# Other orders for the last two batches, and one batch's down projections in another PSUM bank, in a gated cross-attention and expert kernel

## What is computed

```python
def xattn(x, ctx, ...):                     # 16 heads of 8 channels
    y  = softmax(causal(q @ k.T * scale)) @ v        # self attention
    y += softmax(qc @ kc.T * scale) @ vc             # against the context
    return y @ Wp + bp

def ffn(x, ...):                            # 16 experts, hidden size 64
    combine = route(x @ router_weight.T)    # sigmoid, best 2 of 4 groups, best 4 experts, weights
    for e in range(16):
        out += combine[:, e] * ((silu(x @ w_gate[e].T) * (x @ w_up[e].T)) @ w_down[e].T)

x = x + tanh(g_xattn) * xattn(layernorm(x), ctx)
x = x + tanh(g_ffn) * ffn(layernorm(x))
```

## Time and profile before

| | us |
|---|---|
| median of 3 runs | 349.12 |
| the 3 runs | 349.02 to 356.06 |
| the profiled execution | 349.41 |
| its span | 347.6 |
| busy in the span: PE, DVE, ACT, POOL | 318.1, 256.4, 196.2, 151.1 |

### The profile page before, as it was taken

One profiled execution on the slowest core, in us unless ns is written; L12 is line 12 of the kernel. 1 busy time (PEld: TensorE's weight loads), 2 busy tenths in 40 slices (PEclk: granted clock), 3 DMA queues, 4 the chain that ended last, 5 costly groups with the idle time before them and its releaser, 6 DMA issues.

```text
span 347.6 us, 8679 instructions
## 1 busy us (share of the span) xinstructions
PE 318.1 (92%) x3186; PEld 247.7 (71%) x3186; DVE 256.4 (74%) x639; ACT 196.2 (56%) x399; POOL 151.1 (43%) x176
## 2 busy tenths in 40 slices
PE   1579599989999999999999999999999999978696
PEld 0455365666687788778887888787888787856665
DVE  4238666868898888988798888888889854748742
ACT  2433356767667765687637765675666467532041
POOL 3884061404470588047633494318410722903422
PEclk9856759999999999999999999999999999989999
DMA  4269674688563855537655365077156005214000
GB/s 123 68 183 188 146 194 115 145 209 187 199 151 103 184 131 149 143 96 151 147 139 133 88 172 140 20 152 183 34 124 141 0 18 90 37 50 88 16 1 15
DMA packets 32889, 40.45 MB, mean 116 GB/s; under 512 B 3440, under 2 KB 29824, under 8 KB 30368
## 3 DMA queue, kind: packets, MB, share of 16 engines
q1 hardware_dynamic: 32004, 38.46, 46.7%
q10 hardware_dynamic: 844, 1.45, 1.7%
HBM read 29.84 MB, written 7.45 MB: 107 GB/s over the span
## 4 chain that ended last, share of the span: by engine, by line
PE 76%; DVE 7%; DMA 6%; SPq 5%; POOL 2%; issue 2%; ACT 1%; POOLq 0%; DVEq 0%
PE bank L918 15%; PE bank L846 14%; PE bank L825 8%; PE bank L943 7%; PE bank L800 7%; PE bank L803 6%; PE bank L822 5%; DMA k_stack<-tri_k 4%; SPq L427 2%; PE bank L893 2%; DVE row_max L1011 2%; PE bank L861 2%; PE bank L852 2%; SPq L426 1%; PE bank L956 1%
## 5 line engine op out<-in xcount | busy, mean ns | idle before, releaser
L1011 DVE TENSOR_REDUCE row_max<-bank 128x2 f32<-128x512 f32 (+1 forms) x224 | 146.9, 686 | 43.0 <-PE bank L803 24.9
L709 ACT ACTIVATE probs<-bank 128x512 f32<-128x512 f32 x224 | 127.5, 595 | 57.5 <-PE bank L825 27.7
L918 PE MATMUL bank<-xn2T,w_pairs_sb 128*128 128x256 f32 x256 | 68.0, 392 | 1.5 <-issue 0.9
L846 PE MATMUL bank<-probs,v_ext 128*32 128x256 f32 (+1 forms) x1024 | 57.2, 365 | 0.0
L626 POOL TENSOR_TENSOR f_h<-f_h,comb 128x512 f32<-128x512 f32 x32 | 40.3, 1273 | 36.1 <-DMA comb<-c_scr 20.4
L803 PE MATMUL bank<-k_stack,q_stack 72*128 72x256 bf16 x256 | 49.9, 284 | 2.7 <-DVE row_max L1011 2.1
L918 PEld LDWEIGHTS bank<-xn2T,w_pairs_sb 128*128 128x128 f32 x256 | 44.7, 193 | 8.3 <-issue 2.8
L825 PE MATMUL bank<-q_stack,k_stack 73*128 73x256 bf16 x256 | 49.2, 284 | 1.0 <-DMA q_stack<-shiftT 0.9
L412 POOL TENSOR_TENSOR rest<-proj,part 128x512 f32<-128x512 f32 x14 | 16.2, 1160 | 74.7 <-ACT part L682 74.6
L846 PEld LDWEIGHTS bank<-probs,v_ext 128*32 128x32 f32 x1024 | 30.0, 112 | 19.9 <-issue 4.7
L800 PE MATMUL bank<-k_stack,q_stack 121*128 121x128 bf16 (+1 forms) x384 | 39.1, 231 | 2.4 <-DMA k_stack<-tri_k 1.9
(11 more groups left out here) (113 smaller groups left out, 367.9 us busy)
## 6 DMA issues: line engine op xcount, KB each, us to landing
k_stack<-k_scr SPq DMA_DIRECT2D x45, 192.0 KB
q_stack<-q_scr SPq DMA_DIRECT2D x14, 576.0 KB
comb<-c_scr SPq DMA_DIRECT2D x14, 512.0 KB, 6.7
q_scr<-part SPq DMA_DIRECT2D x46, 64.0 KB
k_scr<-part SPq DMA_DIRECT2D x46, 64.0 KB
x_in<-in_x SPq DMA_DIRECT2D x8, 128.0 KB, 2.4
w_pairs_sb<-in_w_pairs SPq DMA_DIRECT2D x1, 1024.0 KB, 7.8
out<-y_out SPq DMA_DIRECT2D x8, 128.0 KB, 1.9
```

The costliest lines, as they stand in the source:

```text
L709: nc.scalar.activation(probs[:, seq % NP, :], exp_bank[s % 2][:, :], ACT.Exp).then_inc(exp_done, 1)
L846: last = pe.matmul(pv_bank[32 * n:32 * n + VW, col + q0:col + T], v[:, VW // 2 * odd:VW // 2 * odd + VW], weights, start=odd == 0 and kt = ...
L918: last = pe.matmul(bank_of[:, n * T:(n + 1) * T], w[:, e0:e0 + 128], xn2T[:, :], start=True, stop=True)
L1011: nc.vector.tensor_reduce(row_max[:, kind, qt, h0:h0 + nh], max_bank[k % 2][:, :].rearrange("p (h k) -> p h k", h=nh), AX.X, ALU.max).then ...
```

## The change

The lists of PE, ACT and DVE are changed from batch 6's routing weights on, and nowhere before. POOL's and SP's lists stay as they are. The down projections of batch 6 go to bank 4, whose last values have by then been copied out, and `out:6` reads them there. `ga:7` therefore no longer waits for `out:6` and can stand ahead of `down:6`. Of `ORDERS` one line of DVE's stands here, and the rows behind the diff show what moves on PE and ACT.

```diff
-        tup:5:3 route:6 route:6:1 route:6:2 route:6:3 m:7 route:6:4 route:6:5 out:5 swish:6 m:7:1 tup:6 swish:6:1
-        tup:6:1 x1:7 stats2:7 swish:6:2 tup:6:2 xnv2:7 swish:6:3 tup:6:3 route:7 route:7:1 route:7:2 route:7:3 out:6
+        tup:5:3 route:6 route:6:1 route:6:2 route:6:3 m:7 route:6:4 route:6:5 out:5 m:7:1 swish:6 tup:6 x1:7 stats2:7 swish:6:1 tup:6:1 swish:6:2 tup:6:2 xnv2:7 swish:6:3 tup:6:3 route:7 route:7:1 route:7:2 route:7:3 out:6
...
+        def down_bank(b):
+
+            return pv_bank if b == B - 2 else gate_bank
...
-                    ge(pe, out_made, b)
+                    ge(pe, out_made, b if b < B - 1 else 0)
...
                 if j == 0:
                     pe.wait_ge(f_gate_done, b * GP + GP)
+                    if b == B - 2:
+                        pe.wait_ge(pv_copied, 2 * B)
...
-                    last = pe.matmul(gate_bank[:, n * 128:(n + 1) * 128], f_h[:, j, n * 128:(n + 1) * 128], w_down[:, j, :],
+                    last = pe.matmul(down_bank(b)[:, n * 128:(n + 1) * 128], f_h[:, j, n * 128:(n + 1) * 128], w_down[:, j, :],
...
-                    nc.vector.tensor_tensor(y_out[:, :, :], gate_bank[:, 0:T].rearrange("p (n c) -> p n c", n=NQ),
+                    nc.vector.tensor_tensor(y_out[:, :, :], down_bank(b)[:, 0:T].rearrange("p (n c) -> p n c", n=NQ),
```

More of the change, by code:

```diff
@@ L143 @@
         exp:7:24 down:5 down:5:1 y:7 down:5:2 down:5:3 exp:7:25 down:5:4 exp:7:26 down:5:5 exp:7:27 down:5:6 down:5:7
-        combT:6 pv:7:3 ga:6 up:6 y:7:1 ga:6:1 yT:7 up:6:1 wp:7 ga:6:2 up:6:2 ga:6:3 up:6:3 xn2T:7 logits:7 down:6
-        down:6:1 down:6:2 down:6:3 down:6:4 down:6:5 down:6:6 down:6:7 ga:7 combT:7 up:7 sprd:7 ga:7:1 up:7:1 sprd:7:1
+        pv:7:3 ga:6 y:7:1 up:6 yT:7
+        ga:6:1 wp:7 combT:6 up:6:1 ga:6:2 up:6:2 ga:6:3 up:6:3 xn2T:7 logits:7 ga:7 down:6
+        down:6:1 down:6:2 down:6:3 down:6:4 up:7 down:6:5 down:6:6 down:6:7 combT:7 sprd:7 ga:7:1 up:7:1 sprd:7:1
         ga:7:2 up:7:2 sprd:7:2 ga:7:3 sprd:7:3 up:7:3 down:7 down:7:1 down:7:2 down:7:3 down:7:4 down:7:5 down:7:6
@@ L180 @@
         exp_e:7:15 tanh:5:2 exp_e:7:16 exp_e:7:17 exp_e:7:18 exp_e:7:19 pv_e:7 exp_e:7:20 tanh:5:3 exp_e:7:21 xn2T_e:6
-        rt:6 exp_e:7:22 exp_e:7:23 exp_e:7:24 exp_e:7:25 exp_e:7:26 exp_e:7:27 combT_e:6 pv_e:7:1 tanh:6 tanh:6:1
-        yT_e:7 tanh:6:2 tanh:6:3 xn2T_e:7 rt:7 tanh:7 combT_e:7 tanh:7:1 sprd_e:7 sprd_e:7:1 tanh:7:2 sprd_e:7:2
+        rt:6 exp_e:7:22 exp_e:7:23 exp_e:7:24 exp_e:7:25 exp_e:7:26 exp_e:7:27 pv_e:7:1 tanh:6 yT_e:7 combT_e:6 tanh:6:1 tanh:6:2 tanh:6:3 xn2T_e:7 rt:7 tanh:7 combT_e:7 tanh:7:1 sprd_e:7 sprd_e:7:1 tanh:7:2 sprd_e:7:2
         tanh:7:3 sprd_e:7:3''',
```

## The result

The changed kernel is slower by 1.3%: the ratio to the kernel before is 1.013, 95% interval 1.010 to 1.016, from 20 runs of each (the medians of all 20 are 354.57 and 350.55 us). The profiled execution of the changed kernel took 354.09 us with a span of 352.3.

A forecast was written before the change was run, and what follows sets the result against it. PE was taken as the bound, with a 1.91 us wait ahead of `combT:6`. Span 347.6 plus 2.4 for `ga:7:1` and 1.2 for the clock made 351.2, hence a median of 352.7 us, range 350.3 to 355.3.

The forecast's parts named there:

- the clock term: PE's idle stretches before the down projections and around `combT:7`: half clock behind one costs 1.2 us, bounds 0 and 2.7.
- the base: Kernel before: profiled execution 349.41 us, 0.3 above the median of the runs, from which the forecast total was reckoned.
- the second rival: On DVE, batch 7's routing runs into POOL's products and ends near 332: 354.5 to 356.0 us, chance 0.13.
- The wait removed: PE ahead of `combT:6`: the 1.91 us wait goes, and attention's last output, `y:7:1`, comes 4.0 us earlier.
- `combT:6` behind `x1:7`: On PE, it waits for bank 7 and starts at 314.3; ACT's copy ends at 315.1, 6.3 us later than before.
- The way through DRAM: Batch 6's routing weights, ACT's copy to landing: 9.2 us as before, no longer hidden, landing at 324.3.
- an even result: Store and two loads of routing weights by the skill's rule: 6.5 us, weights at 321.6, sum about even; rejected for the rows.
- Down projections, `out:6`, `r_w`: Behind POOL's products: down projections end 3.1 us later at 331.1, `r_w` at 332.4, `ga:7:1` starts 2.4 us later at 334.5.
- Routing beside POOL's products: Batch 7's routing on DVE is slowed beside the products but done by 330, ahead of 331.1: nothing on the path.
- The rival that it would not be slower: At POOL's first product of batch 6, the weights come in time: 348.5 to 349.5 us, chance 0.11.

The follow-up runs named there:

- e: The changed kernel with `ga:7`'s four matmuls done three times before their result is signalled, to fill PE's idle time; ratio to before 1.007 (1.001 to 1.013).
- f: The changed kernel without batch 6's two loads of routing weights and POOL's wait for them, output false for batch 6; ratio to before 1.003 (0.998 to 1.008).
- j: The changed kernel with `out:6` behind `tup:7` on DVE and `combT:7` between `down:6:5` and `down:6:6` on PE; ratio to before 1.005 (1.001 to 1.010).
- d: The changed kernel with `combT:6` directly behind `pv:7:3`, `out:6` behind `tup:7`, `combT:7` inside the down projections; ratio to before 0.994 (0.989 to 0.998), repeat 0.994.
- i: Kernel d with `xnv2:7` moved ahead of `swish:6:2` on DVE; ratio to before 0.999 (0.995 to 1.003).
- b: The kernel before with bank 4 for batch 6, `ga:7` ahead of `down:6` and `up:7` inside them, `combT:6` unmoved; ratio to before 1.012 (1.008 to 1.017).
- c: The changed kernel with `combT:6` directly behind `pv:7:3` on PE and its copy moved up on ACT; ratio to before 1.005 (1.000 to 1.010).
- h: Kernel a with `combT:6` directly behind `pv:7:3` and its copy moved up; ratio to before 0.988 (0.980 to 0.996), from two runs.
- g: The kernel before with `pv:7:3` ahead of `combT:6` on PE and their copies swapped on ACT; ratio to before 0.995 (0.991 to 1.000).
- a: The changed kernel with `ga:7` and `up:7` behind `down:6` again and the old bank for the down projections; ratio to before 1.008 (1.003 to 1.012).

## Why the prediction was right or wrong

The sign and the mechanism were right, and the size fell short. The step that failed is the clock term of the sum: I put 1.2 us for it, out of 0 to 2.7, and the runs showed the full 2.7, because the clock fell twice, each time at about the price that I had given it, though the second time not at the place that I had named. The second thing short is the base. Against the profiled execution I forecast 353.0 and it took 354.09; the median of 20 runs is 354.57 against my 352.7. My number hung on the median of three runs, 349.12, and 20 runs of the kernel before have 350.55. Measured from there 352.7 is a loss of 2.1 us, about half of the 4.6 us that the ratio means. As a difference my sum was +3.6, 1.0%, just at the lower end of the interval. The measured time lies where I had put the second rival (354.5 to 356.0), but what that rival says, routing that ends behind the down projections, didn't happen.

- *The wait removed.* Right. `pv:7:3` starts at 305.80 (306.1), `y:7:1` ends at 309.78 (309.8), `x1:7` at 313.92 (314.1).
- *`combT:6` behind `x1:7`.* Right: 313.98 (314.3), ACT's copy ends at 314.78 (315.1).
- *The way through DRAM.* Right: 9.2 us again, landing at 323.96 (324.3), first product at 324.10 (324.45). The Trainium skill's transfer times, by which I estimated an even result (DMA: Bandwidth & Descriptors, Anatomy of one DMA), did not hold for these loads. The Trainium skill gives them for transfers issued by GpSimd, and these are issued from SP. By them a load of 512 KB is an estimated 3.2 us; of the two loads here the one that landed last took 7.1 us from issue, as before.
- *Down projections, `out:6`, `r_w`.* Right in order, late by 0.7: `down:6` ends at 331.85 (331.1), `r_w` at 333.12 (332.4), `ga:7:1` starts at 335.17 (334.5). The half clock in the down projections, which my sum had in its clock term, is 1.05 of it: `down:6` takes 6.35 us from its first record to its end here and 5.30 in e. Without it `ga:7:1` would start at 334.1, 0.4 earlier than I said, mostly because the weights came 0.35 earlier. (PE before wasn't quite without a gap from 324.22 on, as I wrote: it waited 0.91 us for `out:6`. The sum doesn't use that.)
- *Routing beside POOL's products.* As said: `r_glim` 1.23 us, `r_ein` 1.29 for two, `r_etop` 0.83, all done at 328.3, 3.6 us before `out:6`. It cost nothing here.
- *The clock.* This is the term that failed. I took 1.2 us out of 0 to 2.7; it was 2.7: 1.05 in the down projections and 1.66 behind `ga:7:1`, where 13.23 us of before became 14.89. I had priced them at 1.0 and 1.7 and had reasoned that one of two idle stretches would be followed by half clock. The first was; it was also longer than I had worked out, 2.61 us and not 1.9, since `ga:7` ended at 322.9 and not at 323.9. Behind the second, around `combT:7`, the clock held for nine us, and then fell while PE was busy, which no row of before had shown.

So the sum as it came out: 2.0 us for the orders (2.4 forecast) and 2.7 for the clock (1.2 forecast), 4.7 in all (3.6 forecast), which is what the two profiled spans differ by. The 2.0 already has in it that the half clock of before, worth up to 1.7 us, is gone; with no half clock in either kernel the new orders would cost up to 3.7 us.

The rival that it would not be slower fell at the point that I named: POOL started at 324.10, not by 322.0. Kernel f, which takes that wait away, had its `ga:7:1` at 23.59, 0.8 us earlier than before, where I had worked out 0.6. The experiments added what the steps held but I had not priced as a cause of its own: `out:6` ahead of the last words of the routing. With `combT:7` moved too it is 2.3 us of j's gain between the end of `down:6` and `ga:7:1`. Of the kernels that keep the second half of the change, only d and its repeat, with both causes removed, are faster than before, by 0.6% with both intervals below 1; i, which has them removed too, is level with the kernel before.

## What to carry to other kernels

Before a step is moved back to spare its engine a wait, follow all that hangs on its result, DMAs above all: here 1.9 us of waiting were exchanged for 9.2 us of transfers that were no longer hidden, and that cost 3.9 us up to `ga:7:1`. The better move was the smallest one, to let the one step that needn't wait go ahead and leave the waiting step directly behind it. And where a result is needed soon by two chains, the reader of the slower one (`out:6`) should not stand in the list ahead of the last steps of the other.

## What the runs showed of the hardware that I had not expected

From 300 us on, PE was idle for 1.9 us or more once in each of six profiles (1.91, 1.96, 2.33, 2.38, 2.61 and 3.39 us), and half clock came behind each. It also came without: in the down projections of b, c and h behind waits of 1.13 us at most, where d and i stayed at full clock behind waits of up to 0.99 us. And it came with PE busy for the nine us before: from 343.3 in the changed kernel, and likewise in e, f and g near the end of the span, but not in before, a, c, d, h, i and j, whose PE does the same work there. Each such stretch costs 1.6 to 1.7 us in this fully busy part: from `ga:7:1` to the last `out` it is 13.2 us without one, 14.9 with one and 16.4 with two. What sets it off there is open; no run here isolates it. Since it moves an execution by up to 3 us, and the kernels here differ by 2 to 5, the distances between two steps in which the clock was the same say more about an order than the total of one profile.
